# The router's small steps moved from GpSimd to VectorE, in the PSUM bank of the logits

## The reference, cut to what matters

```python
result = jnp.einsum('bsd,od->bso', x, base_w) + base_b
ax = jnp.einsum('bsd,edr->bser', x, lora_A)
bax = jnp.einsum('bser,ero->bseo', ax, lora_B)
logits = jnp.einsum('bsd,ed->bse', x, router_w) + router_b
kth = jax.lax.top_k(logits, TOP_K)[0][..., -1:]
masked = jnp.where(logits < kth, NEG_INF, logits)
expert_weights = jax.nn.softmax(masked, axis=-1)
return result + SCALING * jnp.einsum('bse,bseo->bso', expert_weights, bax)
```

## Time and profile before

| what | value |
|---|---|
| median of 3 runs | 5525.69 us (5523.0 to 5528.63) |
| the profiled execution's own time | 5525.26 us |
| its span, first to last instruction | 5523.5 us |
| mean granted TensorE clock | 0.985 |
| TensorE busy | 5113.2 us, 93% |
| VectorE busy | 4999.6 us, 91% |
| GpSimd busy | 4215.9 us, 76% |
| ScalarE busy | 3967.2 us, 72% |

### The profile page before, as it was taken

How to read it: one execution, slowest core, us unless ns; L and a number is a source line. 1 busy time by engine, 2 the same in 40 slices (tenths; PEclk the granted TensorE clock), 3 DMA queues, 4 the chain that set the end, 5 groups by cost and what they waited for, 6 DMA issues and landing times.

```text
span 5523.5 us, 94525 instructions
## 1 busy us (share of the span) xinstructions
PE 5113.2 (93%) x32280; PEld 3450.1 (62%) x32280; DVE 4999.6 (91%) x7745; ACT 3967.2 (72%) x6278; POOL 4215.9 (76%) x2641
## 2 busy tenths in 40 slices
PE   4799999999999999999999999999999999999996
PEld 2466666666666666666666666666666666666664
DVE  3999999999999999999999999999999999999983
ACT  2677777777777777777777777777777777777763
POOL 2778777887777887777877777888777888777772
PEclk7899999999999999999999999999999999999998
DMA  4444554444555454554444555444554445554440
GB/s 127 140 145 149 153 161 153 146 148 147 155 161 152 142 151 148 156 161 152 142 148 151 154 163 149 143 148 148 153 166 149 142 148 147 155 167 147 144 141 28
DMA packets 521455, 812.22 MB, mean 147 GB/s; under 512 B 80432, under 2 KB 227288, under 8 KB 520976
## 3 DMA queue, kind: packets, MB, share of 16 engines
q1 hardware_dynamic: 513072, 805.79, 48.3%
q10 hardware_dynamic: 7904, 0.39, 0.1%
HBM read 716.50 MB, written 88.38 MB: 146 GB/s over the span
## 4 chain that ended last, share of the span: by engine, by line
PE 44%; DVE 32%; issue 12%; ACT 5%; DMA 3%; POOL 1%; SPq 1%; ACTq 1%; DVEq 0%; POOLq 0%
DVE pD L1207 10%; DVE mx L1256 7%; PE pY L945 7%; PE pM L967 5%; DVE state L1207 4%; PE pM L1076 4%; DVE state L1215 4%; PE pM L1020 3%; DMA bc<-bc_d 3%; PE pM L1051 3%; DVE xc L1247 3%; PE pM L954 2%; PE pM L1002 2%; PE pM L1073 2%; PE pM L1125 2%
## 5 line engine op out<-in xcount | busy, mean ns | idle before, releaser
L575 POOL TENSOR_TENSOR state<-scan_in,bc 128x1024 f32<-128x1024 f32 x1024 | 2412.0, 2365 | 687.1 <-PE pY L945 439.6
L1207 DVE TENSOR_TENSOR_SCAN pD<-pD,state 128x512 f32<-128x512 f32 x1536 | 1849.0, 1217 | 76.3 <-POOL state L575 38.1
L714 ACT ACTIVATE pD<-scan_in,A 128x512 f32<-128x512 f32 x2048 | 1393.6, 688 | 584.0 <-DVE state L1215 482.3
L945 PE MATMUL pY<-ident,state 128*128 128x128 f32 x8192 | 1142.1, 276 | 12.1 <-POOL state L563 7.7
L945 PEld LDWEIGHTS pY<-ident,state 128*128 128x128 f32 x8192 | 912.1, 142 | 260.1 <-issue 172.5
L1215 DVE TENSOR_TENSOR state<-pD,bc 128x512 f32<-128x512 f32 x1536 | 1024.4, 681 | 42.1 <-DMA bc<-bc_d 27.7
L813 ACT ACTIVATE region<-pM 128x512 f32<-128x512 f32 (+1 forms) x1408 | 754.7, 555 | 327.9 <-PE pM L1053 292.5
L1256 DVE TENSOR_REDUCE mx<-pM 128x1 f32<-128x512 f32 (+3 forms) x1408 | 859.7, 630 | 130.0 <-PE pM L1035 127.8
L563 POOL TENSOR_TENSOR state<-state,bc 128x512 f32<-128x512 f32 x512 | 645.5, 1273 | 268.7 <-DVE state L1207 263.5
L1207 DVE TENSOR_TENSOR_SCAN state<-pD,state 128x512 f32<-128x512 f32 x512 | 611.5, 1210 | 78.2 <-ACT pD L714 78.2
L1033 PE MATMUL pM<-region 96*128 96x512 bf16 (+3 forms) x2048 | 527.9, 303 | 120.8 <-DVE mx L1256 73.6
(11 more groups left out here) (167 smaller groups left out, 8041.8 us busy)
## 6 DMA issues: line engine op xcount, KB each, us to landing
bc<-bc_d SPq DMA_DIRECT2D x2048, 256.0 KB, 4.0
region<-qk_d SPq DMA_DIRECT2D x640, 128.0 KB, 3.1
qk_d<-qkp SPq DMA_DIRECT2D x64, 384.0 KB, 3.5
qk_d<-ht SPq DMA_DIRECT2D x64, 384.0 KB, 2.7
xt<-in_x_dram SPq DMA_DIRECT2D x32, 512.0 KB, 5.2
region<-qk_d SPq DMA_DIRECT2D x256, 64.0 KB, 2.7
hres_d<-xt SPq DMA_DIRECT2D x32, 512.0 KB, 4.5
x<-hres_d SPq DMA_DIRECT2D x32, 512.0 KB, 5.5
```

The source lines that it names most:

```text
L575: nc.gpsimd.tensor_tensor(state[:, at_:at_ + JP], us[:, parity(b), k // N * JP:(k // N + 1) * JP, :], bc[:, k % BC_SLOTS, 0, :].unsqueeze( ...
L714: act.activation(pD[DECAY_BANK[e]][:], dts[:, parity(b), j], ACT.Exp, scale=A[:, j, n:n + 1]).then_inc(a_ok.sem, 1)
L945: ins = pe.matmul(y_part(t, e % JP), state[:, e % RING, t * P:(t + 1) * P], ident[:], is_transpose=True, start=False, stop=(e % PASS >= PA ...
L1207: v.tensor_tensor_scan(h if e in POOL_C else decay, decay, h, 0.0, ALU.mult, ALU.add)\
```

## The change

The three GpSimd steps of the router go. VectorE takes them over, and works in the PSUM bank of the logits (bank 3), which is cut into four parts of 32 columns: the logits (biased in place), the 0/1 mask, the shifted logits, and the masked exponentials. The four comparisons become one instruction over all tiles, the memset goes. ScalarE reads the shifted logits from PSUM. The bank is released to TensorE by `ew_ok`, the end of the normalisation, in place of `rt_c`. VectorE's `esum` moves from behind `qk2` to a place ahead of `mx1_10`.

```diff
--- before.py
+++ after.py
@@ -278,10 +278,7 @@
         mx = sb("mx", [P, 2, 16])
         mrow = sb("mrow", [16, 2, P], BF16)
         rden = sb("rden", [P, TB, G])
-        lg = sb("lg", [P, TB, E])
         top = sb("top", [P, TB, 8])
-        keep = sb("keep", [P, TB, E])
-        lgs = sb("lgs", [P, TB, E])
         ew = top
         esum = sb("esum", [P, TB])
 
@@ -342,7 +339,7 @@
         xr_in, modg_in, modf_in, x2_ok = sig("xr_in", 16), sig("modg_in", 48), sig("modf_in", 16), sig("x2_ok", 2)
         n3, h3_ps, h3_ok = sig("n3", TB), sig("h3_ps", KT), sig("h3_ok", KT)
         rt_ps, rt_c, ex_ok = sig("rt_ps", 1), sig("rt_c", 5), sig("ex_ok", 1)
-        rk_ok, kp_ok, wk_ok, es_ok, ew_ok = (sig("rk_ok", 1), sig("kp_ok", TB), sig("wk_ok", 1), sig("es_ok", 2),
+        rk_ok, kp_ok, wk_ok, es_ok, ew_ok = (sig("rk_ok", 1), sig("kp_ok", 1), sig("wk_ok", 1), sig("es_ok", 2),
                                              sig("ew_ok", 1))
         la_ps, ax_ok, axt_ps, axt_ok = sig("la_ps", 1), sig("ax_ok", 1), sig("axt_ps", 1), sig("axt_ok", 1)
         xb_ok = sig("xb_ok", 1)
@@ -370,6 +367,11 @@
             for name, shift in order:
                 if shift < 0:
                     step(name, Batch(None, B - 1))
+
+        def router_parts():
+
+            parts = pM[bank_of("route")][:, 0:4 * TB * E].rearrange("p (c t e) -> p c t e", t=TB, e=E)
+            return parts[:, 0], parts[:, 1], parts[:, 2], parts[:, 3]
 
         def parity(b):
             return b.off % 2
@@ -625,21 +627,6 @@
                     nc.gpsimd.tensor_tensor(xr, xr, nrm(b), ALU.add).then_inc(x2_ok.sem, 1)
                 elif name == "l3s":
                     rstd(b, 3)
-                elif name == "route":
-
-                    b.wait(pool, rt_c)
-                    nc.gpsimd.tensor_tensor(lgs[:], lg[:], top[:, :, 0:1].broadcast_to([P, TB, E]), ALU.subtract)\
-                      .then_inc(rk_ok.sem, 1)
-                elif name == "wkeep":
-
-                    b.wait(pool, ex_ok)
-                    b.wait(pool, kp_ok)
-                    nc.gpsimd.tensor_tensor(ew[:], ew[:], keep[:], ALU.mult).then_inc(wk_ok.sem, 1)
-                elif name == "wnorm":
-
-                    b.wait(pool, es_ok)
-                    nc.gpsimd.tensor_tensor(ew[:], ew[:], esum[:].unsqueeze(2).broadcast_to([P, TB, E]), ALU.mult)\
-                      .then_inc(ew_ok.sem, 1)
                 elif name == "xb":
 
                     b.wait(pool, n3)
@@ -861,7 +848,7 @@
                 elif name == "route2":
                     b.wait(act, rk_ok)
                     b.wait(act, kp_ok)
-                    act.activation(ew[:], lgs[:], ACT.Exp).then_inc(ex_ok.sem, 1)
+                    act.activation(ew[:], router_parts()[2], ACT.Exp).then_inc(ex_ok.sem, 1)
                 elif name in ("out0", "out1"):
                     n = int(name[3])
                     b.wait(act, out_ps, n + 1)
@@ -1101,7 +1088,7 @@
                     b.wait(pe, n3)
                     turned(name, lambda t: nrm(b)[:, t, k * P:(k + 1) * P], h3_ps, b, h3_ok, k + 1)
                 elif name == "route":
-                    ps = next_bank(name, b, rt_c, 1, (h3_ok, KT))
+                    ps = next_bank(name, b, ew_ok, 1, (h3_ok, KT))
                     for t in range(TB):
                         for k in range(KT):
                             ins = pe.matmul(ps[:, t * E:(t + 1) * E], h2T[:, k, t * P:(t + 1) * P], w_rt[:, k, :],
@@ -1304,23 +1291,30 @@
                 elif name == "route":
 
                     b.wait(dve, rt_ps)
-                    v.tensor_tensor(lg[:], pM[bank_of(name)][:, 0:TB * E].rearrange("p (t e) -> p t e", e=E),
-                                    rb_row[:].unsqueeze(1).broadcast_to([P, TB, E]), ALU.add)\
+                    logits, kept, shifted, _ = router_parts()
+                    v.tensor_tensor(logits, logits, rb_row[:].unsqueeze(1).broadcast_to([P, TB, E]), ALU.add)\
                      .then_inc(rt_c.sem, 1)
 
                     b.wait(dve, rt_c, 1)
-                    v.memset(held[:], 0.0)
                     for t in range(TB):
-                        v.max(top[:, t, :], lg[:, t, :]).then_inc(rt_c.sem, 1)
+                        v.max(top[:, t, :], logits[:, t, :]).then_inc(rt_c.sem, 1)
 
                     b.wait(dve, rt_c, 5)
-                    for t in range(TB):
-                        v.tensor_scalar(keep[:, t, :], lg[:, t, :], top[:, t, 1:2], None, ALU.is_ge).then_inc(kp_ok.sem, 1)
+                    v.tensor_tensor(shifted, logits, top[:, :, 0:1].broadcast_to([P, TB, E]), ALU.subtract)\
+                     .then_inc(rk_ok.sem, 1)
+                    v.tensor_tensor(kept, logits, top[:, :, 1:2].broadcast_to([P, TB, E]), ALU.is_ge)\
+                     .then_inc(kp_ok.sem, 1)
                 elif name == "esum":
+                    _, kept, _, weighed = router_parts()
+                    b.wait(dve, ex_ok)
+                    v.tensor_tensor(weighed, kept, ew[:], ALU.mult).then_inc(wk_ok.sem, 1)
                     b.wait(dve, wk_ok)
-                    v.tensor_reduce(esum[:], ew[:], AX_X, ALU.add).then_inc(es_ok.sem, 1)
+                    v.tensor_reduce(esum[:], weighed, AX_X, ALU.add).then_inc(es_ok.sem, 1)
                     b.wait(dve, es_ok, 1)
                     v.reciprocal(esum[:], esum[:]).then_inc(es_ok.sem, 1)
+                    b.wait(dve, es_ok, 2)
+                    v.tensor_tensor(ew[:], weighed, esum[:].unsqueeze(2).broadcast_to([P, TB, E]), ALU.mult)\
+                     .then_inc(ew_ok.sem, 1)
                 elif name == "lora":
                     b.wait(dve, la_ps)
                     b.wait(dve, ew_ok)
@@ -1359,9 +1353,9 @@
     "POOL": """
...
-        -l3s +ql0 fill15 fill16 pc30 -xb +ql1 -route -wkeep fill17 -wnorm pc31 +ql2 fill18 fill19 -gb -put fill20
...
+        -l3s +ql0 fill15 fill16 pc30 -xb +ql1 fill17 pc31 +ql2 fill18 fill19 -gb -put fill20 fill21 pc38 pc39 fill22
...
@@ -1395,14 +1389,14 @@
...
-        mx1_10 c32 +qk2 -esum scan33 -lora mt1 scan34 c33 c34 +qk3 scan35 scan36 c35 mx2_0 c36 gate0 scan37 mx2_1
+        -esum mx1_10 c32 +qk2 scan33 -lora mt1 scan34 c33 c34 +qk3 scan35 scan36 c35 mx2_0 c36 gate0 scan37 mx2_1
...
```

More of the change, by code:

```diff
@@ L1361 @@
         fill7 fill8 +l0s fill9 pc14 pc15 +l0a fill10 +l0b fill11 +l0c fill12 pc22 +l1s fill13 pc23 -x2 -x2b fill14
-        -l3s +ql0 fill15 fill16 pc30 -xb +ql1 -route -wkeep fill17 -wnorm pc31 +ql2 fill18 fill19 -gb -put fill20
-        fill21 pc38 pc39 fill22 fill23 fill24 +ql3 fill25 pc46 pc47 fill26 fill27 fill28 fill29 pc54 pc55 fill30
-        fill31 +u0 +fill0 +u1 pc62 pc63 +fill1 +fill2 +fill3 +fill4 +pc6 +pc7 +fill5 l2s +fill6 f1_0
+        -l3s +ql0 fill15 fill16 pc30 -xb +ql1 fill17 pc31 +ql2 fill18 fill19 -gb -put fill20 fill21 pc38 pc39 fill22
+        fill23 fill24 +ql3 fill25 pc46 pc47 fill26 fill27 fill28 fill29 pc54 pc55 fill30 fill31 +u0 +fill0 +u1 pc62
+        pc63 +fill1 +fill2 +fill3 +fill4 +pc6 +pc7 +fill5 l2s +fill6 f1_0
     """,
@@ L1401 @@
         scan49 mx3_6 mx3_7 c48 c49 mx3_8 scan50 mx3_9 c50 mx3_10 scan51 mt3 c51 scan52 c52 scan53 c53 scan54 scan55
-        scan56 scan57 c56 c57 on1 scan58 +mx0_0 on2 +mx0_1 scan59 +mx0_2 c58 +mx0_3 c59 scan60 c60 scan61
-        c61 scan62 scan63 +scan0 +scan1 on3 gate1 +c0 +c1 +mx0_4 +scan2 +c2 +scan3 +scan4 +c3 +c4 +scan5 +c5
-        +scan6 +scan7 +scan8 +scan9 sso0 +c8 sso1 l2s +c9 +mx0_5 +scan10 +c10 +scan11 +mx0_6 +c11 +mx0_7 +scan12
-        +mx0_8 +scan13 +c12
+        scan56 scan57 c56 c57 on1 scan58 +mx0_0 on2 +mx0_1 scan59 +mx0_2 c58 +mx0_3 c59 scan60 c60 scan61 c61 scan62
+        scan63 +scan0 +scan1 on3 gate1 +c0 +c1 +mx0_4 +scan2 +c2 +scan3 +scan4 +c3 +c4 +scan5 +c5 +scan6 +scan7
+        +scan8 +scan9 sso0 +c8 sso1 l2s +c9 +mx0_5 +scan10 +c10 +scan11 +mx0_6 +c11 +mx0_7 +scan12 +mx0_8 +scan13
+        +c12
     """,
```

## The result

The changed kernel takes 5647.5 us (median of 4 runs, 5642.5 to 5652.6) against 5526.0 of the kernel before: a ratio of 1.0221, 95% interval 1.0206 to 1.0236. It is slower by 121 us, where 50 were forecast and 5590 was the top of the range.

A forecast was written before the change was run, and what follows sets the result against it. The prediction took the chain through VectorE's first router step and mx1_9's maxima to TensorE's st0_1_3 as the bound. 30 x 1.69 us, plus 1.07, less 0.7, gave +51.1 on 5525.26: 5576 us, range 5562 to 5590.

The forecast's parts named there:

- The chain and its hand-over: Waits run through VectorE's first router step and mx1_9's maxima to TensorE at st0_1_3, with no slack behind it on TensorE.
- VectorE's first step: Router comparisons become two instructions over all tiles and the memset goes; the step shrinks by some 0.4 us.
- rival 1: Faster: the wait on bank 3 is hidden, the shorter first step gains 12 us, giving 5513 us; chance 3%.
- The exponential and the four steps: From T, the bias add's start: exponential at T+1.42; product, sum, reciprocal and normalisation on VectorE done at T+2.51.
- The fixed extra in the Trainium skill's table: Three instructions now reading the PSUM bank would take 0.065 us more each, 6 us over all batches; not adopted.
- the pitch of 0.22 us in the sum: Start-to-start time taken for dependent small VectorE steps behind the exponential, from bias add to first maximum.
- The new wait: Bank 3 is free for mx1_10 only after the normalisation: start T+2.55 in place of T+0.32, T being the bias add's start.
- +1.69 us per batch: Delay on the chain: st0_1_3 starts 3.68 us after the bias add's start in place of 1.99.
- the 51 us of the sum: Total forecast slowdown: 30 x 1.69 = 50.7 us, batch 30 adding 1.07, last batch gaining 0.7; together +51.1 us.
- they follow at their pace: 0.47 + 0.22 + 0.44 = 1.13 us: On TensorE behind the late mx1_10, st0_1_2, add29 and st0_1_3 keep their old spacing, so st0_1_3 starts 1.13 us later.
- rival 3: TensorE's clock falls from 2.4 to 1.2 GHz after the stop; slower LoRA matmuls add 57 us, giving 5633; chance 3%.

The follow-up runs named there:

- e2: Kernel before with bank 3 released by wk_ok, GpSimd's product with the mask, in place of the bias add; no step moved: 5598.4 us, ratio 1.0138.
- e6: Kernel before with shifted logits and mask written from PSUM to SBUF by VectorE, bank released by the mask, e3's TensorE order: 5517.9 us, ratio 0.9991.
- e10: e6 with dec33 ahead of qk2 in ScalarE's order: 5515.3 us, ratio 0.9980 to the kernel before.
- e1: Changed kernel with two more fp32 matmuls into the free bank 1 ahead of mx1_10, their result overwritten: 5582.4 us, ratio 1.0108 to the kernel before.
- e9: Changed kernel with mx1_10 behind lora on TensorE, mt1 behind add30, partners moved along, mt1 ahead of c33 on VectorE: 5538.6 us, ratio 1.0019.
- e3: Changed kernel with st0_1_2 and add29 ahead of mx1_10 in TensorE's order: 5558.6 us, ratio 1.0063 to the kernel before.
- e4: Kernel before with all small router steps on VectorE in an SBUF tile, bank released by the bias add, esum behind qk2: 5647.4 us, ratio 1.0223.

## Why the prediction was wrong

- **The chain and its hand-over** (`mx1_9` to `st0_1_3`, no slack behind it): right. e2, with nothing but the release changed, slows a batch by the full 1.2 us wherever the clock stays up.
- **VectorE's first step**: right. It was to shrink by 0.4 us and did (T+1.25 to T+0.84). The 30 x 0.4 = 12 us of rival 1 are not shown to be its worth alone: with the hold out of the way it brought 5 us (e6), and the 12 came only with another order on ScalarE (e10).
- **The exponential and the four steps**: right, T+1.41 against T+1.42 and T+2.49 against T+2.51. The instructions out of PSUM took 0.19 to 0.20 us against 0.17 for the sum out of SBUF before. The fixed extra in the Trainium skill's table (VectorE: DVE Perf Modes, section on the TRN2 errata) would be 0.065; the trace shows 0.02, and the pitch of 0.22 us in the sum was the measured one.
- **The new wait**: right in place and start, `mx1_10` at T+2.55. The term "+1.69 us per batch" was a little small. In e1, at full clock, the period from router 0 to router 29 is 167.84 us against 166.05, so 1.79 more, and 0.1 of that is `lora`, which is late by 0.1 us more than `st0_1_3` because it waits for late exponentials. Against the 51 us of the sum e1 measures 60. Of the 9 over it, 3 are this 0.1 per batch and 4 lie ahead of the first router, where no router step has run yet; the rest stays open.
- **The term that was missing: the clock.** The step that failed is "they follow at their pace: 0.47 + 0.22 + 0.44 = 1.13 us" together with the 3% for rival 3. They followed at half the clock, in 2.11 us, and part of `lora` did too. e1 puts this at 61 us. Rival 3 was the right case, 15 us short of 5647.5. That its price of 57 us came so near is partly luck: it doubled `lora` in every batch and nothing else, while in the two batches shown the 1.13 us came to 2.1, and `lora` took 3.73 us in one of them and 2.37 in the other, against 2.00 at full clock.
- **Why it got 3%.** I weighed it by one row, a stretch with TensorE busy for 2.38 of 4.00 us at a clock of 1.00. Within it the longest single stop was 1.6 us, and the new one was to be 2.2. One row in which the clock held was taken as a proof for a longer stop. The trace of the kernel before has a stop of the new length too, once, in the first turn of the lists, and there the clock fell. The stop inside the window of the earlier trace rows, and then that one, the work behind it and the clock from 201 to 207 us:

```profile
2593.30 0.39 PE L1033 MATMUL pM<-region 96*128 96x512 bf16 x1 [1.60 <-DVE mx L1256]
```

```profile
199.90 0.28 PE L1033 MATMUL pM<-region 96*128 96x256 bf16 x1 [2.18 <-DVE xc L1247]
...
201.11 1.06 PE L945 MATMUL pY<-ident,state 128*128 128x128 f32 x4
```

```profile
201.00:207.00 6.00, 5.42 (x13) 2.55 (x12) 6.00 (x9) 3.41 (x7) 4.04 (x4) 0.50 0.11 39
```

The add takes the same 1.06 us as in the kernel after. These rows were there to be read before the change was run, with the price of the steps at the lower clock. With them rival 3 would have weighed at least as much as the forecast. That one fall was no accident: a stop of 2.17 to 2.18 us at this place is in the profiles of all twelve kernels, and the clock falls behind it in eleven, in all but e9.

The Trainium skill's rule (TensorE: Matmul & The Clock Gate, Part 1), that the clock follows how busy the engine has just been, agrees with e1, e2 and e3 by the rows above.

## What to carry to other kernels

A PSUM bank used as scratch space is held from the first write to the last read, and the price is paid by whoever fills it next, with everything queued behind; a change of one release signal, with no work moved (e2), cost 76 us. When a wait on TensorE grows beyond any stop that the profile shows at full clock, put the matmuls behind it at both clock levels into the sum, and before dropping the idea look for steps in the queue that could run ahead of the wait: two of them (e3) recovered 85 of 121 us. Look for a stop of the new length anywhere in the profile of the kernel before, the start of the program included, and read the clock behind it. Small steps that have two inputs in SBUF beside a busy GpSimd are no way out (e4).

## What the runs showed of the hardware

- Two matmuls that compute nothing of use made a kernel 61 us faster (e1, from 121 to 60 us above its own runs of before), with the granted clock between the routers at 1.00 and not 0.98 on average.
- The fall of the clock is not a fixed property of a stop: in e2 a stop of about 1.6 us per batch left the clock at 1.00 in 15 of 30 batches and not in the other 15, and its runs scatter over 26 us, those of the kernel before over 6. In the kernel before 29 stops of 1.6 us between 190 and 5310 us left it at 1.00. Stops of 1.92 to 2.36 us lowered it 30 times out of 30 in the kernel after, stops of 3.0 us 24 times out of 30 in e4.
- The same VectorE instruction on 32 numbers took 0.19 us at the end of the program, where GpSimd was idle, and 2.15 us in the median beside GpSimd's fills, when both inputs were in SBUF (e4); with one of them in PSUM it took 0.20 us throughout, though GpSimd had work at the same time (kernel after).
- In e4 the clock fell as well (mean 0.976 against 0.985), so its 125 us are not those of the long instructions alone: 80 by the start of `st0_1_3`, and the other 45 were not separated.
